# A decoder layer on one core: routed rows are stored, weighed and gathered in another order, and the weights' store moves from SyncE's queue to ScalarE's

## The reference, cut to what matters

```python
router_probs = softmax(x @ gate_w + gate_b)                    # 8 experts
expert_values, expert_indices = top_k(router_probs, k=2)
expert_values = expert_values / (sum(expert_values) + 1e-09)
shared = gelu(x @ sh_w1 + sh_b1) @ sh_w2 + sh_b2               # every token, 256 -> 1024 -> 256
moe = sum over the 2 chosen e: weight_e * (gelu(x @ ew1[e] + eb1[e]) @ ew2[e] + eb2[e])
out = layernorm(x + shared + moe)
```

## Time and profile before

| | |
|---|---|
| median of three runs | 864.14 us |
| the profiled execution: time, span | 863.78 us, 862.5 us |
| mean granted clock of TensorE | 0.999 of full speed |
| busy share of the span: PE, DVE, ACT, POOL | 98%, 70%, 64%, 45% |
| feed-forward routing, around the change | about 576 to 623 us of the span |
| experts' tiles | about 622 to 835 us of the span |

### The profile page before, as it was taken

One profiled execution on the slowest core, in us unless ns is written; L12 is line 12 of the kernel. 1 busy time (PEld: TensorE's weight loads), 2 busy tenths in 40 slices (PEclk: granted clock), 3 DMA queues, 4 the chain that ended last, 5 costly groups with the idle time before them and its releaser, 6 DMA issues. The chain is left out here.

```text
span 862.5 us, 22785 instructions
## 1 busy us (share of the span) xinstructions
PE 845.4 (98%) x8040; PEld 672.9 (78%) x8040; DVE 602.3 (70%) x1638; ACT 548.5 (64%) x1219; POOL 387.2 (45%) x493
## 2 busy tenths in 40 slices
PE   8999999999999999999999999999899999999996
PEld 7888888888888888867666666676688888888864
DVE  6586779776668675756666666888666666666655
ACT  7888877867676776655656655655345555554555
POOL 4543534352433475425534433445535454444433
PEclk9999999999999999999999999999999999999999
DMA  9853424334234333300000000199575555554326
GB/s 314 227 174 121 148 103 144 133 114 148 99 118 128 106 116 58 99 1 2 1 1 1 2 1 1 35 382 370 180 161 79 76 78 78 77 71 87 57 26 201
DMA packets 83626, 93.14 MB, mean 108 GB/s; under 512 B 38559, under 2 KB 69343, under 8 KB 83391
## 3 DMA queue, kind: packets, MB, share of 16 engines
q1 hardware_dynamic: 75487, 80.90, 30.6%
q0 software_dynamic: 7488, 10.27, 8.8%
q10 hardware_dynamic: 544, 0.52, 0.2%
HBM read 56.00 MB, written 30.56 MB: 100 GB/s over the span
## 5 line engine op out<-in xcount | busy, mean ns | idle before, releaser
L667 POOL TENSOR_SCALAR prob<-prob,rden 128x128 f32<-128x128 f32 (+1 forms) x256 | 123.0, 499 | 159.3 <-DVE rden L989 159.3
L2316 PE MATMUL ps<-slots,e 128*128 128x128 f16 x1248 | 124.2, 219 | 0.0
L870 ACT ACTIVATE prob<-prob,nmx 128x128 f32<-128x128 f32 (+1 forms) x256 | 113.2, 446 | 8.6 <-DVE nmx L983 8.6
L2324 PE MATMUL ps<-e,xT 128*128 x312 | 117.2, 379 | 0.0
L2402 ACT ACTIVATE slots<-slots 128x512 f32<-128x512 f32 x78 | 49.1, 630 | 105.8 <-DVE slots L2447 95.0
L2316 PEld LDWEIGHTS ps<-slots,e 128*128 x1248 | 100.9, 97 | 19.1 <-issue 0.2
L2285 POOL DMA_INDIRECT back_y<-xs,dst x39 | 67.5, 1730 | 96.1 <-DMA back_y<-xs,dst 55.2
L983 DVE CUSTOM_DVE_ANT_0 prob<-ps,mask 128x128 f32<-128x128 f32 (+1 forms) x256 | 73.7, 353 | 35.0 <-PE ps L755 34.8
L31 PE MATMUL ps<-xT,wqkv 128*128 128x256 f16 x768 | 94.7, 273 | 0.4 <-ACT slots L877 0.3
L2325 PE MATMUL ps<-e,xT 128*128 x312 | 85.0, 273 | 0.0
L31 PEld LDWEIGHTS ps<-xT,wqkv 128*128 128x128 f16 x768 | 72.1, 98 | 15.3 <-issue 5.9
(11 more groups left out here) (279 smaller groups left out, 1897.6 us busy)
## 6 DMA issues: line engine op xcount, KB each, us to landing
halves<-parted SPq DMA_DIRECT2D x36, 512.0 KB, 2.9
piece<-in_L_ffn_ew SPq DMA_DIRECT2D x32, 512.0 KB, 4.5
e<-halves SPq DMA_DIRECT2D x16, 1024.0 KB, 13.8
piece<-in_L_ffn_sh_w SPq DMA_DIRECT2D x4, 512.0 KB, 10.2
sw<-halves SPq DMA_DIRECT2D x4, 512.0 KB, 6.5
xs<-back_y SPq DMA_DIRECT2D x8, 256.0 KB, 5.0
out<-xs SPq DMA_DIRECT2D x8, 256.0 KB, 2.2
xs<-in_x SPq DMA_DIRECT2D x1, 1536.0 KB, 12.5
```

The source lines that it names most:

```text
L667: PO.tensor_scalar(prob[u][:, h, r], prob[u][:, h, r], rden[u][:, h, t:t + 1], 1.0, ALU.mult, ALU.mult).then_inc(normed, 1)
L870: SC.activation(at, at, ACT.Exp, bias=nmx[u][:, h, t:t + 1], scale=-1.0, accum_out=den[u][:, h, t:t + 1]).then_inc(exped, 1)
L2316: yield PE.matmul(ps[:, 2 * u + q, (k % 4) * P:(k % 4) * P + P], w[ch][h], xgT[i % TURNED][:, j * DC + ch, :], start=n == 0, stop=n == 3 * ...
L2324: yield PE.matmul(ps[:, 4 + u, :], he[u][0][:, k, :], w, start=k == 0, stop=False, skip_group_check=True)
```

## The change

Four edits go together.

1. Token part 4 counts its landing on `stored` (used otherwise only by the output's stores at the end); `STORED`, the count of parts on `x_stored`, goes from 3 to 2. All that needs every token waits for `stored` as well; `part_choices(0)` waits for parts 2 and 3 alone.
2. `weigh_choices` is cut in two: its first four instructions move from behind `part_choices(1)` to a place between `count_tokens` and `place_rows`; the last three stay, as `scale_choices`.
3. `store_weights` moves from SyncE to ScalarE, behind the gelu and high half of block 17.
4. The first two gathers move on GpSimd from behind `hidden_low(20)` and `hidden_low(21)` to behind `hidden_low(19)` and `hidden_low(20)`.

```diff
-        TURNED, ROUTED, STORED = 3, 7 * I, 3
+        TURNED, ROUTED, STORED = 3, 7 * I, 2
-            GATHER_AT = (20, 21)
+            GATHER_AT = (19, 20)
 def store_tokens(k):
-                             parts.bitcast(F32)).then_inc(x_early[k] if k < 2 else x_stored, 16)
+                             parts.bitcast(F32)).then_inc((*x_early, x_stored, x_stored, stored)[k], 16)
 def store_weights():
-                SY.wait_ge(x_stored, 16 * STORED)
-                SY.wait_ge(w_line, WEIGHED)
-                SY.dma_start(rows_x[P:P + T, D:D + 2].rearrange("(t p) k -> p t k", p=P), top_w,
+                SC.wait_ge(x_stored, 16 * STORED)
+                SC.wait_ge(w_line, WEIGHED)
+                SC.dma_start(rows_x[P:P + T, D:D + 2].rearrange("(t p) k -> p t k", p=P), top_w,
                              allow_slow_non_contiguous=True).then_inc(x_stored, 16)
 def ffn_sync():
-                store_weights()
                 turn_rows(0)
 ...
                 SY.wait_ge(x_stored, 16 * STORED)
+                SY.wait_ge(stored, 16)
 def ffn_pool():
                     if m in GATHER_AT:
                         PO.wait_ge(r_line, NAMED)
                         PO.wait_ge(x_stored, 16 * (STORED + 1))
+                        PO.wait_ge(stored, 16)
                         gather(GATHER_AT.index(m))
 def ffn_scalar():
+                    if m == 17:
+                        store_weights()
 def weigh_choices():
                 VE.scalar_tensor_tensor(s1, p2, TOP_EPS, s2, ALU.add, ALU.add).then_inc(w_line, 1)
+
+            def scale_choices():
+
                 VE.wait_ge(w_line, 4)
                 VE.reciprocal(r0, s1).then_inc(w_line, 1)
 def shared_base(g):
                 if g == NG - 1:
                     VE.wait_ge(x_stored, 16 * STORED)
+                    VE.wait_ge(stored, 16)
 def ffn_vector():
                     if m == 12:
                         count_tokens()
+                        weigh_choices()
                         place_rows()
                     if m == 14:
-                        weigh_choices()
+                        scale_choices()
 def combine_sync():
-                SY.wait_ge(stored, 16 * CHUNKS)
+                SY.wait_ge(stored, 16 + 16 * CHUNKS)
```

## The result

The changed kernel takes 866.54 us (median of 22 runs, 863.77 to 868.11); beside them the kernel before took 863.79 us (22 runs). The ratio is 1.0029, 95% interval 1.0021 to 1.0036, so +2.5 us (1.8 to 3.1). The forecast was +1.3 us, 865.3 us, with a range of 859.8 to 868.4. The profiled execution took 867.39 us, with a span of 866.1 us and a mean granted clock of 0.996. All of this trace lies 0.9 us later than the trace before already ahead of the change (the store of part 1 is issued at 575.9 instead of 575.0); subtract that when rows are compared.

What follows compares the result with a forecast made beforehand. TensorE, busy 98%, was taken to bound the kernel through the experts' start: 2.8 us gained, 5.2 and 0.5 lost less 1.49 replaced, so +1.3 us. Forecast 865.3 us, range 859.8 to 868.4, own range 864.3 to 866.8.

Steps and rivals of the forecast that it cites:

- What bounds, and where: TensorE, busy 98%: experts' tiles run without a break, so their start sets the end; waits before them give at most 4.28 us.
- Part 4 apart, and the weighing in two: VectorE's tables: the 0.99 us wait goes, four weighing instructions worth 1.8 us move into a 1.52 us gap.
- both waits gone, 2.8 us (2.3 to 2.8): TensorE's waits before table products 0 and 2 both go, so block 20 starts 2.8 us sooner.
- ScalarE's store: Weights' store on ScalarE's queue: packets take turns with the loads, so the weights land at 612.6, as before.
- The gathers a block sooner: On GpSimd, hidden_low(20) queues behind gather 0, which waits for the weights; TensorE stands 5.2 us, and 0.5 us later.
- The sum: Gained 2.8 us, lost 5.2 and 0.5 less 1.49; experts at 623.6 instead of 622.32, end 1.3 us later.
- later start, +1.3: Experts' tiles on TensorE start at 623.6 instead of 622.32, and the end moves by the same 1.3 us.
- The clock (18%): Rival, 18%: TensorE's clock falls to 1.2 GHz in the pause before down(20), costing 3 us: 868.3 us.
- The early landing (25%): Rival, 25%: on ScalarE's queue the weights land early; from 607.4 all three TensorE waits go, 859.9 us.
- break-even: The weights' landing time, 611.4 us, at which the change neither gains nor loses; later or earlier moves it one for one.
- Part 3 no sooner than part 4: Rival, 7%: the tables aren't released and 0.62 us stays before table 0; 865.3 to 866 us.
- a dearer mix of packets: Rival, 3%: mixing small and large packets costs extra, or loads are delayed; landing 614 to 615, 867 to 868 us.

Runs made afterwards that it cites:

- e8: The kernel before with only SyncE's order changed: the weights' store ahead of the last three loads of experts' weights; 864.46 us, ratio 1.0006.
- e6: e4 with the two gathers back behind hidden_low(20) and hidden_low(21); 864.99 us, ratio 1.0017 to the kernel before.
- e9: e4 with SyncE turning tile 1 right behind tile 0, ahead of the first two base stores; 862.05 us, ratio 0.9982 to the kernel before.
- e10: e6 with SyncE turning tile 1 ahead of the first two base stores; 861.10 us, ratio 0.9975 to the kernel before.
- e11: e8 with SyncE turning tile 1 ahead of the first two base stores; 863.17 us, ratio 0.9999 to the kernel before.
- e2: The changed kernel with the weights' store back on SyncE, behind the experts' loads; 866.13 us, ratio 1.0029 to the kernel before.
- e4: The changed kernel with the weights' store on SyncE ahead of the last three loads of experts' weights; 861.48 us, ratio 0.9971 to the kernel before.
- e1: The changed kernel with the two gathers back behind hidden_low(20) and hidden_low(21); 863.62 us, ratio 1.0002 to the kernel before.
- e5: The kernel before with only the two gathers moved ahead, behind hidden_low(19) and hidden_low(20); 865.67 us, ratio 1.0026.
- e3: The changed kernel with 14 matmuls whose result nobody reads ahead of down(20), in the pause; 865.19 us, ratio 1.0019 to the kernel before.
- e7: The changed kernel with the weights' store on SyncE ahead of the last load of experts' weights only; 862.49 us, ratio 0.9992 to the kernel before.

## Why the prediction was right, and where it was not

- **What bounds, and where.** Right in the main. But I had taken the experts' tiles for "TensorE itself without a break", so that only their start counts. The traces of the changed kernel and of the others have breaks there: 0.3 to 0.7 us ahead of tile 1 in eleven, 2.28 us in e8, and in e6 and e9 waits of 1.85 and 1.00 us as late as 634 us.
- **Part 4 apart, and the weighing in two.** Right in kind: the 0.99 us wait and the 0.62 us are gone, the four instructions fit in the gap. The term "both waits gone, 2.8 us (2.3 to 2.8)" was too large: it is 2.0 us, below its range. I had named VectorE's meetings with GpSimd, and then counted "some tenths"; the trace has 1.0 us in L2171 and 1.0 in L2119. That the two edits can be worth 2 us in time, e10 against e11 shows.
- **ScalarE's store.** Right, the step on which the direction hung. Packets by turns, 203 to 211, last packets after the loads, landing at 612.3 (forecast 612.6). The first packet went out 3.6 us behind the issue and not at once; as the last ones wait for the loads in any case, this changed nothing. e2 shows that the queue makes no difference to the time; e4 that the place ahead of the loads does. The Trainium skill ("Trainium Kernel Development and Optimization", Key Constraints) has DMAs of several engines share the same 16 engines, with only issue time to be saved; these runs agree, with 866.5 and 866.1 us. The Trainium skill's other rule, turns of typically 9 to 17 descriptors ("DMA: Bandwidth & Descriptors", Queues, rings and completion order), is not what q1 and q10 show here: one packet record each.
- **The gathers a block sooner.** Right: `hidden_low(20)` behind the gather, TensorE waiting for it; the times of e1 and e5 show from both sides that this edit makes the loss. The pause was 3.6 us, not 5.2: TensorE arrived 0.9 us less early, the weights landed 0.4 us sooner, and the gather took 1.46 instead of 1.78 us. The further 0.5 us in front of `down(22)` didn't come.
- **The sum.** The direction came out, with half the size (+1.3 against +2.5, 1.8 to 3.1), but the terms did not. I had 2.8 us gained, 5.7 us lost less 1.49, the experts 1.3 us later, and nothing else. The changed kernel's trace, on the scale of before, has 2.0 gained and 3.6 lost less 1.5. The clock comes on top: from `down(20)` to the experts TensorE needs 8.4 us (616.76 to 625.20), where the same blocks take 6.8 us in e2's trace (614.52 to 621.28). So of the 2.0 us by which the experts start later, 1.7 are the clock's and only some 0.3 the waits'. The first two tiles add 0.9 us that the prediction put at nothing. e3's trace agrees: no later start, 0.9 us in these tiles. The term "later start, +1.3" was too large by 1 us and the missing one made up for it; that 865.3 lies near the 864.8 of the runs with a steady clock and near e3's 865.2 is partly luck.
- **The clock (18%).** This rival came true, and by the prediction's own sign ("I am wrong if ... the granted clock dips near 616") the forecast was wrong there, though 866.54 lies in its own range of 864.3 to 866.8. The fall comes in 18 of 22 runs. I had its price at 3 us; it is 2.2 us by the runs (867.0 against 864.8) and 1.7 us in the trace. I had held it unlikely because 2.17 us of waiting left the clock at 1.00 in the trace before; but that was one execution, a third of the runs of the kernel before have a lower mean clock, and e5 shows one and the same kernel with either.
- **The early landing (25%).** It didn't happen; made to happen, it gives 861.5, not 859.9. The break-even that I gave, 611.4 us, wasn't tried closer than e7's 609.3 (862.5 us).
- **Part 3 no sooner than part 4** didn't happen (L2167 at 593.87 without a wait), nor did a dearer mix of packets.

## What to carry to other kernels

Before a wait is moved ahead on an in-order engine, ask what lands last for it and what is then queued behind it: here one line moved `hidden_low(20)` behind a landing, and alone it cost nearly as much as the whole change (e5). A small store behind large loads isn't freed by another queue; it is freed by its order, issued ahead of the last loads that nobody needs yet. And a pause of TensorE of some microseconds can cost more than its length, since the clock may fall in it. A sum of waits up to one point holds only if what follows runs as before; here the first two tiles behind it didn't, and only the traces, not the time, could tell.

## What the runs showed of the hardware that I had not expected

- Filling 3.0 us of a 3.6 us pause with matmuls that nobody reads kept the clock in all of 11 runs and made the kernel about 0.9 us faster (1.0019 against 1.0029, the intervals overlap).
- The weights' first packet went out only at 604.97 us, 3.6 us behind its issue on ScalarE's queue at 601.39, and in e1 and e3 it is 3.6 to 3.7 us too. Over 601.4 to 604.5 us the changed kernel's queues have this one line only:

```profile
q1 hardware_dynamic: 330, 1.27, 102.6%
```

- Gathers from GpSimd's queue moved no packet in 608 to 612 us beside full-rate loads, though two were issued by 610.4 us.
- VectorE instructions that meet a GpSimd instruction stretch by up to 1 us (1.22 to 2.18 us in L2171), or it is GpSimd's that stretches (2.11 us at 594.40, against 1.16, where L2171 kept its 1.22). That they hold each other is read from the traces alone; no kernel was made to test it.
